# The last part's stage order, from spans and weights to a written-out string, in an eight-sequence attention, FFN and windowed top-k kernel on one core

## The reference, cut to what matters

```python
x = x + attn_a(layernorm(x))      # 16 heads of 8, softmax over all 1024 keys
x = x + ffn(layernorm(x))         # 256 -> 512 -> 512 -> 128 with +1/-1 weights
x = x + attn_b(layernorm(x))      # see below
x = x + ffn(layernorm(x))         # the same weights again
```

```python
kw = q_h[:, idx, :]                                  # the 64 tokens up to this one
dist = sqrt((((kw - q_h[:, :, None, :]) ** 2) * metric).sum(-1) + 1e-08)
neg, loc = top_k(-dist, 32)                          # the 32 nearest of 64
infl = exp(-topd); infl = infl / (infl.sum(-1) + 1e-08)
context = einsum('btk,btkd->btd', infl, v_h[loc]) + gate * 0.1 * (qhat @ Hm)
out = (q_h * context) @ decoder
```

## Time and profile before

| what | value |
|---|---|
| median of 3 runs | 2957.09 us |
| lowest and highest run | 2952.42 and 2960.92 us |
| the profiled execution, first to last instruction | 2956.4 us |
| LAST, in that execution | 2678 to 2956.4 us |
| busy in the whole span | PE 82%, ACT 76%, DVE 71%, POOL 25% |

### The profile page before, as it was taken

One profiled execution on the slowest core, in us unless ns is written; L12 is line 12 of the kernel. 1 busy time (PEld: TensorE's weight loads), 2 busy tenths in 40 slices (PEclk: granted clock), 3 DMA queues, 4 the chain that ended last, 5 costly groups with the idle time before them and its releaser, 6 DMA issues.

```text
span 2956.4 us, 60895 instructions
## 1 busy us (share of the span) xinstructions
PE 2416.3 (82%) x21171; PEld 1045.7 (35%) x21171; DVE 2096.8 (71%) x10258; ACT 2258.2 (76%) x3159; POOL 732.5 (25%) x933
## 2 busy tenths in 40 slices
PE   4788778888788887888888887888878888888666
PEld 1112233244332443334422443324433344324444
DVE  5801768957787668966799577876679666992585
ACT  4798668977699677987789776996769877895543
POOL 3020115211251114401162112511134111321442
PEclk6599789999899999999999998999989999999887
DMA  3011001100011001210011000110012000000000
GB/s 88 30 49 40 2 19 48 50 18 6 23 56 43 18 10 27 65 31 9 19 44 54 18 6 23 54 42 17 6 26 74 31 9 13 11 20 1 16 20 12
DMA packets 98519, 84.79 MB, mean 29 GB/s; under 512 B 19955, under 2 KB 79541, under 8 KB 98213
## 3 DMA queue, kind: packets, MB, share of 16 engines
q1 hardware_dynamic: 97968, 80.41, 9.3%
q10 hardware_dynamic: 244, 0.49, 0.1%
HBM read 55.32 MB, written 25.44 MB: 27 GB/s over the span
## 4 chain that ended last, share of the span: by engine, by line
PE 34%; ACT 34%; DVE 18%; issue 6%; POOL 6%; SPq 2%; DMA 1%; ACTq 0%; DVEq 0%; POOLq 0%
PE banks L849 31%; ACT PT L1188 17%; DVE xn L1535 4%; ACT pq L1175 3%; DVE h L1538 3%; DVE pq L1322 2%; ACT hparts L1199 2%; POOL Aop L820 2%; ACT h L1200 2%; ACT xn L1133 2%; PE banks L856 2%; ACT h L1101 1%; ACT Bs L1101 1%; POOL qkf L761 1%; DVE stat L1296 1%
## 5 line engine op out<-in xcount | busy, mean ns | idle before, releaser
L1188 ACT ACTIVATE PT<-banks 128x1024 f32<-128x1024 f32 x1024 | 996.6, 1038 | 51.0 <-PE banks L849 47.4
L1322 DVE CUSTOM_DVE_ANT_0 pq<-pq,banks 128x512 f32<-128x512 f32 x1024 | 653.5, 684 | 182.5 <-ACT pq L1175 182.0
L1175 ACT ACTIVATE pq<-banks 128x1024 f32<-128x1024 f32 x512 | 522.9, 1022 | 226.2 <-PE banks L849 201.0
L849 PE MATMUL banks<-PT,Vg 128*9 128x512 f32 x4096 | 545.0, 604 | 2.2 <-ACT PT L1188 2.2
L849 PE MATMUL banks<-Q,K 51*128 51x512 bf16 x2048 | 391.7, 393 | 139.7 <-ACT PT L1188 113.4
L849 PE MATMUL banks<-K,Q 48*128 48x512 bf16 x2048 | 361.6, 431 | 84.8 <-ACT pq L1175 38.0
L801 POOL TENSOR_TENSOR hparts<-h,hparts 128x512 fp32r<-128x512 f32 x108 | 135.6, 1272 | 995.2 <-ACT h L1200 995.2
L1535 DVE MATCH_REPLACE8 xn<-h,xn 128x96 f32<-128x96 f32 x1536 | 354.3, 256 | 0.0
L849 PE MATMUL banks<-hparts,W 128*128 128x512 f32 x992 | 291.4, 421 | 35.0 <-ACT h L1200 24.4
L849 PEld LDWEIGHTS banks<-Q,K 51*128 51x128 bf16 x2048 | 96.4, 93 | 619.1 <-ACT PT L1188 526.8
L1538 DVE MAX8 h<-xn 128x8 f32<-128x96 f32 x1536 | 264.3, 251 | 0.0
(11 more groups left out here) (217 smaller groups left out, 3330.6 us busy)
## 6 DMA issues: line engine op xcount, KB each, us to landing
Vw<-scratch_v SPq DMA_DIRECT2D x256, 51.0 KB, 2.1
scratch_k<-pq SPq DMA_DIRECT2D x24, 384.0 KB, 3.1
K<-scratch_k SPq DMA_DIRECT2D x126, 72.0 KB
qkf<-in_hidden_states SPq DMA_DIRECT2D x16, 512.0 KB, 4.4
scratch_q<-pq SPq DMA_DIRECT2D x24, 256.0 KB, 2.3
Q<-scratch_q SPq DMA_DIRECT2D x126, 48.0 KB
K<-scratch_k SPq DMA_DIRECT2D x126, 48.0 KB
scratch_v<-Bs SPq DMA_DIRECT2D x8, 544.0 KB, 3.6
```

Source lines behind the costliest of these rows:

```text
L849: return pe.matmul(o, l, r, start=start, stop=stop)
L1175: act.activation(cut(g), ring_pair if work is TURN0 and g % 2 else pair[0], ACT.Relu).then_inc(diff_out.sem, 1)
L1188: act.activation(PT[:, at:at + 2, :], pair[g % ESLOTS], ACT.Exp, scale=1.0 if i % 8 < 4 else -1.0).then_inc(probs.sem, 1)
L1322: dve.tensor_tensor_reduce(r, r, pair[1 + g % 2][:, par, :], 1.0, -3.0e38, ALU.subtract, ALU.max, mred[:, par, i, qt:qt + 1]).then_inc(max ...
```

## The change: the order of LAST is written out

`tail()` makes the same list as before and then passes it through `woven`. That keeps each side's own sequence of stages and takes the sides in the order of a string of 386 letters. Only the interleaving of `o`, `p`, `q` and `z` in LAST is different. No instruction is added or taken away, and the turns before LAST are the same.

```diff
+def letter(work):
+
+    side, stage = work[:2]
+    if side == "a":
+        return dict(max="m", mrow="m", mturn="t", v="v", exp="x", pvs="s", pvo="s", residual="r")[stage]
+    return "l" if stage == "load" else side
+
+
+def woven(letters, order):
+
+    lines = {}
+    for work in order:
+        lines.setdefault(letter(work), deque()).append(work)
+    out = [lines[at].popleft() for at in letters if at in lines]
+    assert not any(lines.values()) and len(out) == len(order)
+    return out
...
+ORDER_END = (
+    "oooooooooooooooopoopoopooooppppppppppppppppppppppppqqppppppppppppppppppppppppppppppppppppppppppppppppppppppppp"
...
     order = opening() + merged(along(0.250, 0.342, "p", met), along(*TAIL_SPANS["t"], "p", SLOTS_T),
...
                                along(1.0, 1.1, "z", SLOTS_Z[1]))
+    order = woven(ORDER_END, order)
```

More of the change, by code:

```diff
@@ L9 @@
+from collections import deque
 from contextlib import ExitStack
@@ L239, in opening @@
     return first + [("p",) + x for x in rest]
+ORDER_END = (
+    "oooooooooooooooopoopoopooooppppppppppppppppppppppppqqppppppppppppppppppppppppppppppppppppppppppppppppppppppppppp"
+    "qppqpppppppppqqqpqqqqppppqppqqqpqqppqpqqpppppqqpppqpqqqpppqpppqqqpqqqqqqpppqpppppqppppppppqqpppppqqppqqqqqpqpqpp"
+    "qqqpppqppqppqqpppqpqqpqppqppppppppppppppppzpppzzppzpzpzzzppppzppppzpzpzzpppppppppqzzzzppppzzzzppppppzpzpzzzzpzpz"
+    "zppzppppppppppppppzzzzzzzzzzzzzzzzzzzzzzzzzpzzzzzz")
 def tail():
```

## The result

| | us |
|---|---|
| before, median of 4 runs | 2955.90 (2952.42 to 2960.92) |
| after, median of 4 runs | 2933.73 (2928.30 to 2939.02) |
| ratio | 0.9936, 95% interval 0.9915 to 0.9957 |
| profiled execution of after | span 2937.3, its own time 2939.02 |

The kernel is faster, by 22.2 us between these medians. The forecast was 2944 and its range began at 2938, so the sign was right and the size too small.

What follows compares the result with a forecast made beforehand. DVE was taken to set the pace in LAST's eight search rounds (busy 129.2 of 143.3 us). Gains 6.8 + 0 + 3.1 + 1.2 + 0.9 + 0 + 0.8 = 12.8 us off 2956.4 gave 2944 us, range 2938 to 2953.

Steps and rivals of the forecast that it cites:

- 2678 us of the span don't change: Turns before LAST: same instructions in the same order, so only the 278 us behind them can change.
- the forecast for a median is 2944: Whole kernel: profiled span 2956.4 less 12.8 gives 2943.6, taken as 0.7 below the median; 0.43% less.
- Round 0: First search round: `q`'s first norm leaves and the wait for `lnr` goes, round 1 starts sooner; gain 6.8 us.
- `fcd` ahead of round 2: Moved `fcd` meets `fc`, done at 2807.3 as DVE asks at 2807.4: 0, or a 2.2 us loss at low clock.
- Round 2: DVE's waits of 1.80 us for `pv` 1 and 1.30 for `dec` 1 go: gain 3.1 us, from 1.5.
- Round 3: Rounds 3 and 4 were said to differ by places that change no wait.
- first rival: The wait moves rather than goes: gain 4.5 to 8 us, 2948 to 2952 us; chance 0.22.
- Round 5, 6 and 7: Gains of 1.2 us (wait for `pv` 4), 0.9 (`pv` 5) and 0 (`fc` 4, upper bound 1.3).
- The front: Ahead of the rounds: `turn` 6 ahead of `ln` brings `lnT` sooner; gain 0.8 us, from 0 to 1.6.
- The second: Full clock also in rounds 5 and 7 ends waits for `pv` 4 (2.3 more) and `fc` 4 (1.3): 2940 us; chance 0.15.
- The third: The new order says nearly the same, DVE merely waits elsewhere: 2956 ± 3 us; chance 0.08.
- the fourth: Slower: DVE stuck at `fcd` heading round 2, chain to `fc` 12 us longer at half clock; up to 2966 us; chance 0.05.

Runs made afterwards that it cites:

- first pair: First profiles of the kernels before and after, without edits: LAST 275.3 and 260.6 us.
- second pair: Profiles of before_again and after_again, both kernels repeated without edits: LAST 272.9 and 258.3 us.
- norm_alone: Kernel before with only `q`'s first norm (ln, lnr, lnf, lnn) moved into the first FFN: ratio 1.0006, LAST 274.7 us.
- norm_back: Kernel after with `q`'s first norm put back ahead of `lnT` of `q`'s first half: ratio 0.9990, LAST 269.8 us.
- lnf_later: Kernel after with `lnf` and `lnn` of `q`'s second half one search mark later: ratio 0.9941, LAST 258.3 us.
- before_again: Kernel before, unchanged, timed against itself: ratio 0.9989, LAST 272.9 us.
- head_only: New order up to stage 251 of 386 (front, rounds 0 to 3), old order behind it, against the kernel before: ratio 0.9946, LAST 260.7 us.
- tail_only: Old order up to stage 251 of 386, new order behind it, against the kernel before: ratio 0.9992, LAST 270.3 us.
- filled: Kernel after with 117 unused 128x512 products added on PE in 16 places of LAST: ratio 0.9929, LAST 252.6 us.
- after_again: Kernel after, unchanged, timed again against the kernel before: ratio 0.9945, LAST 258.3 us.
- front_back: Kernel after with the old order in its first 29 stages: ratio 0.9965, LAST 261.0 us.

## Why the prediction was off

**The step that failed** is the first one, "2678 us of the span don't change", and with it the last, "the forecast for a median is 2944". It put at nothing how much that time scatters. The instructions there are the same, but their time isn't: LAST began at 2681.1 in the profile of before and at 2676.6 in that of after. I took the profiled execution and a median of three runs as if they fixed that part, and drew the range from the terms of LAST alone. A spread of 16 us in LAST's start is wider than that whole range. Over 29 runs the same kernel had a median of 2949.91, so the three-run median stood 7 us higher; whether by chance or by the chip that it ran on isn't shown. 4.4 of the 19.1 us between the two profiles are of this kind. With this base and the forecast gain of 12.8 the result would have been put at 2937.1; with the measured gain of 14.6, at 2935.3, beside 2933.73 in 4 runs and 2935.75 in 8. With the base of 2957.09 even the true gain gives 2942.5, inside the range, so it is the base that failed and not the gain.

One more slip is in the base, without weight. Where a profiled execution has both, its time is 1.7 to 1.8 us above its span, so that of before took some 2958.1 us (an estimate), 1.0 above the median and not 0.7 below it. 2957.09 less 12.8 is 2944.3 all the same.

**The sum** was also 1.8 us short, which is less than two profiles of one kernel differ. The stretches between the starts of DVE's products (L1542, L1569) of successive rounds, before less after, in the first pair of profiles and in the second:

| up to | forecast | first pair | second pair |
|---|---|---|---|
| `hebb` | 0.8 | -0.1 | 1.6 |
| product 0 | 6.8 | 7.2 | 7.0 |
| product 1 | 0 | -0.1 | 0.1 |
| product 2 | 1.8 | 2.4 | 2.5 |
| product 3 | 1.3 | 0.0 | 0.4 |
| product 4 | 0 | 0.0 | 0.0 |
| product 5 | 1.2 | 2.2 | 0.7 |
| product 6 | 0.9 | 1.0 | 2.1 |
| product 7 | 0 | 1.4 | 0.1 |
| the end | 0 | 0.7 | 0.1 |
| sum | 12.8 | 14.7 | 14.6 |

- **Round 0** held, step by step: the search straight behind `ln`, `lnf` after two pairs, one hold, of 1.36 us where 1.4 was forecast, the mask 3.0 us ahead of round 1 where 3.2 was. norm_alone and norm_back show what the prediction didn't say: its two causes only pay together. It also left out that the old order spent 10 us of this round at half clock and the new one none; the round came out right without that, since it had ACT's evictions, and not PE, set the pace of the four `fa`.
- **`fcd` ahead of round 2** held: 0.16 us where the two were to meet. lnf_later shows that this place is the next limit.
- **Round 2** held, with 0.6 more: I had kept L1553's hold of 0.75 us, as POOL had "an L801 there in either order", and that was wrong: the L828 come later, at 2815.30, and the hold went. **Round 3** was mis-sized by 1.3 us: `dec` 1's wait went, but `aop` 4 on POOL behind two L828 made `dist` 4 late, and `pv` 2's division waits 1.00 us in its place. The prediction had said that rounds 3 and 4 "differ by places that change no wait", though its first rival named that place as one of three that meet within 0.3 us.
- **Round 5, 6 and 7**: forecast 2.1 together, measured 4.6 in the first pair and 2.9 in the second. `pv` 4's wait ended at 1.01 or 2.25, and `fc` 4's of 1.32 was gone in before_again already. head_only and tail_only show that the order has a share in them (2.4 us with the same head). What differs from one execution to the next goes with the clock; filled shows that for `pv` 4. Round 7 gave 1.4 in the first pair, just past the bound of 1.3, and 0.1 in the second.
- **The front**: 0.8 forecast with 0 to 1.6 as its range, some 1.5 to 4 us in most executions. The clock goes with it: over the same 16 us of LAST (8 to 24 us in) it was 0.79 in after_again and 0.57 in front_back. But it was 0.68 in the first profile of after as in both of before, and there the front gave nothing.
- **The rivals.** The second, more than I counted by a higher clock, is the nearest: in the first pair `pv` 4's wait lost 2.5 us and `fc` 4's all of its 1.3, most of what it named. The first came once (round 3), at a price of 1.3. The third is refuted, and so is the fourth: the chain to `fc` 0 ran at full clock (1.00 from 2767.2 to 2842.0).

## What to carry to other kernels

Before a forecast of half a per cent is put beside a median, ask how much the unchanged part scatters: here 16 us in 2670, more than the change is worth, and LAST's own length, which scatters by 2.4, showed the size of the gain best. When a stage is moved out of a busy engine, follow what the engine waits for next: `q`'s norm alone took 0.3 to 0.4 us from the stretch between `hebb` and round 0's product (24.3 or 24.4 to 24.0), and with the `fa` products moved as well it got 7 shorter. Where an engine's waits come from a low clock on PE, another order moves them about, and work for PE in its gaps shortens them.

## What the runs showed of the hardware

- The same stretch ran at different granted clocks in different executions of one kernel: 0.84 and 0.92 over LAST's first 44 us, and `hebb` 4.1 us apart.
- PE waited 6.14 us for `aop` 1 and then stood at a granted 0.50 for 10 us; with `lnT` and `fa` in that wait it stayed at 1.00.
- 117 products without a use raised the mean granted clock in LAST from 0.87 to 0.97 and made it 5.7 us shorter, at 19.6 us more of busy time on PE.
- A DVE instruction with two SBUF inputs and 4 elements a partition took 1.36 us beside POOL's L828 and ended within 0.02 us of it, where 0.16 is usual; the searches beside the same L828 (MAX8 reads one input, MATCH_REPLACE8 has its eight values loaded ahead) took 1.37 and 0.24, as elsewhere. The Trainium skill ("SBUF — State Buffer", Who interferes with whom) draws the line there: a DVE instruction with two SBUF inputs contends with a GpSimd instruction that reads SBUF, one with at most one input doesn't, and the pair of ports that they share is locked and not divided. The trace agrees with both halves of it.
- It goes the other way too. The eight `aop` instructions of a tile of LAST took 4.15 to 4.30 us on POOL wherever a product of a round on DVE (two SBUF inputs, 0.96 us) fell among them, and at most 3.64 wherever none did, in all 14 profiles. `aop` 4 is one of those, with 4.16 us after and 4.21 before.
